# Value products a pair ahead of the sums over ones, and 59 pairs whose two addends TensorE adds, in an adaLN-attention-FFN kernel on one core

## What is computed

```python
def rational_softmax(scores, eps=EPS):
    num = 0.5 * (1.0 + scores * jax.lax.rsqrt(1.0 + scores * scores))
    return num / (jnp.sum(num, axis=-1, keepdims=True) + eps)
...
probs = rational_softmax(scores, EPS)
out = jnp.einsum('bhts,bhsd->bhtd', probs, v)
```

## Time and profile before

| | us |
|---|---|
| runs | 1978.49, 1980.25, 1984.89 |
| median | 1980.25 |
| the profiled execution | 1986.66 |
| its span, first to last instruction | 1984.9 |
| TensorE, VectorE, ScalarE, GpSimd busy | 1735.6, 1755.3, 1715.3, 1688.1 |
| mean granted clock of TensorE | 0.95 of full |

### The profile page before, as it was taken

The page is one execution under the profiler, slowest core; times in us unless marked ns, Lnnn a source line. Parts: engine busy times, 40 slices in busy tenths (PEclk is TensorE's granted clock), DMA queues, the critical chain, the costliest instruction groups (busy, mean ns, idle before and its releaser), DMA issues.

```text
span 1984.9 us, 29603 instructions
## 1 busy us (share of the span) xinstructions
PE 1735.6 (87%) x10668; PEld 884.6 (45%) x10671; DVE 1755.3 (88%) x1762; ACT 1715.3 (86%) x1853; POOL 1688.1 (85%) x720
## 2 busy tenths in 40 slices
PE   8898889998999889988988899889798887998786
PEld 6454346444555345633443444334343334443342
DVE  3988999899898988988899999898799988889887
ACT  2989999899898888999889998899889998899827
POOL 3878898889788878989889998899788988899875
PEclk9989999899899989989999999899999989999898
DMA  5322211322232333421421212212122213111155
GB/s 153 89 79 72 70 56 44 98 65 62 87 84 81 95 97 93 119 62 40 133 56 54 66 53 54 69 50 55 53 53 65 56 34 88 34 44 43 37 208 191
DMA packets 135326, 150.89 MB, mean 76 GB/s; under 512 B 32876, under 2 KB 76908, under 8 KB 134892
## 3 DMA queue, kind: packets, MB, share of 16 engines
q1 hardware_dynamic: 134604, 148.21, 26.5%
q10 hardware_dynamic: 576, 0.79, 0.2%
HBM read 57.44 MB, written 36.45 MB: 47 GB/s over the span
## 4 chain that ended last, share of the span: by engine, by line
PE 35%; ACT 24%; DVE 21%; issue 11%; SPq 4%; POOL 3%; DMA 2%; DVEq 0%; POOLq 0%; ACTq 0%
ACT yb L989 9%; DVE gb L1359 8%; PE sc L1196 7%; DVE gb L1431 7%; ACT yb L991 7%; PE ov L1171 6%; ACT gb L954 6%; PE dn L1171 5%; SPq L586 3%; PE it L1089 3%; PE it L1085 3%; PE it L1122 2%; PE it L1061 2%; PE it L1052 1%; PE sc L1199 1%
## 5 line engine op out<-in xcount | busy, mean ns | idle before, releaser
L911 POOL TENSOR_TENSOR yb<-yb 128x1024 f32<-128x1024 f32 x544 | 1495.9, 2761 | 252.1 <-DVE gb L1431 235.9
L1431 DVE TENSOR_TENSOR gb<-sc,yb 128x1024 f32<-128x1024 f32 x544 | 661.9, 1217 | 152.7 <-ACT yb L991 150.2
L1359 DVE TENSOR_TENSOR gb<-gb,yb 128x1024 f32<-128x1024 f32 x544 | 772.9, 1421 | 0.2
L989 ACT ACTIVATE yb<-sc 128x1024 f32<-128x1024 f32 x544 | 550.8, 1012 | 184.8 <-PE sc L1196 74.0
L1196 PE MATMUL sc<-qmv,kst 128*128 128x512 f32 (+3 forms) x1280 | 468.5, 448 | 154.3 <-DVE gb L1431 152.0
L991 ACT ACTIVATE yb<-yb 128x1024 f32<-128x1024 f32 x544 | 575.7, 1058 | 17.3
L954 ACT ACTIVATE gb<-gb 128x1024 f32<-128x1024 f32 x544 | 566.3, 1041 | 0.0
L1196 PEld LDWEIGHTS sc<-qmv,kst 128*128 128x128 f32 x1280 | 224.3, 198 | 458.6 <-DVE gb L1431 321.7
L1171 PE MATMUL ov<-gb,vv 128*32 128x512 f32 (+3 forms) x2560 | 319.1, 582 | 20.0 <-DVE oT L1379 14.5
L1171 PE MATMUL dn<-gb,ones 128*32 128x512 f32 (+3 forms) x2560 | 306.9, 562 | 0.0
L1085 PE MATMUL it<-hT,wT 128*128 128x512 f32 x488 | 238.9, 608 | 1.2 <-ACT area L966 1.2
(11 more groups left out here) (147 smaller groups left out, 1148.3 us busy)
## 6 DMA issues: line engine op xcount, KB each, us to landing
qmv<-stage SPq DMA_DIRECT2D x378, 64.0 KB
kst<-stage SPq DMA_DIRECT2D x372, 64.0 KB
area<-in_x_dram SPq DMA_DIRECT2D x50, 256.0 KB, 3.0
wf_d<-area SPq DMA_DIRECT2D x21, 256.0 KB, 2.0
wT<-wf_d SPq DMA_DIRECT2D x21, 256.0 KB, 3.0
h_d<-area SPq DMA_DIRECT2D x16, 256.0 KB, 3.3
hT<-h_d SPq DMA_DIRECT2D x4, 1024.0 KB, 7.2
o_d<-oT SPq DMA_DIRECT2D x4, 1024.0 KB, 6.7
```

What stands on the lines that cost most here:

```text
L911: pool.tensor_tensor(y, y, y, ALU.mult).then_inc(s_y2, 1)
L989: act.activation(yview(n), sc[:, n % SLOTS], ACT.Square).then_inc(s_s2, 1)
L1359: dve.tensor_tensor(gview(n), gview(n), yview(n), ALU.add).then_inc(s_num, 1)
L1431: dve.tensor_tensor(gview(n), sc[:, n % SLOTS], yview(n), ALU.mult).then_inc(s_g, 1)
```

## The change

1. `products` is split in two events: the value products "ov" stand at LAG = 5 pairs behind a unit's last pair, the sums over ones "dn" one pair later, where both stood. REGROUP, INVERT, ROWS and NORM are one more each, so that what hangs on dn keeps its pair.
2. A new function `by_load` picks pairs (TWICE) at least 8 apart, where its table of VectorE's work three pairs later is heaviest. The description says 58 of 544; the built program has 59. In these VectorE makes no sum: GpSimd writes y^2 into a buffer of its own, `square`, and TensorE multiplies both gb and `square`, accumulating both in the bank. The ring gb has 7 buffers, and `square` takes the place of the eighth.
3. `scored(k)` on VectorE and GpSimd comes at the next "qk" in any case, so VectorE's `hand_out` stands ahead of the product of its pair.
4. ScalarE waits for the square instead of the sum where the pair four back is in TWICE. The pieces of x1 that are loaded at the end are in another order: tiles 10 to 15 early, 0 to 5 and 6 to 9 late (before: 0 to 5 early, then 6 to 11 and 12 to 15).

```diff
-GRING = 8
+GRING = 7
 NUM_LAG = 2
-LAG = 6
-REGROUP = 1
-INVERT = 2
-ROWS = 3
-NORM = 6
+LAG = 5
+REGROUP = 2
+INVERT = 3
+ROWS = 4
+NORM = 7
+APART = 8
+BEFORE = 3
...
+        sums_at = {(k + 1) % n_pairs: u - n_units * ((k + 1) // n_pairs if u >= 0 else 0) for k, u in product_at.items()}
...
+            if k in sums_at:
+                self.events.append(("dn", sums_at[k]))
             if k in product_at:
-                self.events.append(("pv", product_at[k]))
+                self.events.append(("ov", product_at[k]))
...
+def by_load(groups):
+
+    weight = {"q": 1.4, "k": 1.4, "w2": 1.8, "fb": 0.4, "rt": 0.0, "a": 0.0, "zt": 0.0}
+    n_pairs = len(groups[0].pairs)
+    load = [0.0] * (len(groups) * n_pairs + LAG + 2)
+    for i, g in enumerate(groups):
+        for e in g.events:
+            if e[0] == "qk":
+                k = i * n_pairs + e[1]
+            elif e[0] == "item":
+                load[k] += weight.get(e[1].name[0], 0.65)
+                load[k + 1] += 0.7 * (e[1].name[0] == "zt")
+            elif e[0] == "step":
+                load[k] += 0.7 * (e[1].name[0] == "c8")
+        for last in g.last:
+            load[i * n_pairs + last + LAG + 1] += 1.3
...
+        best[n] = max(best[n + 1], load[n + BEFORE] + 0.3 + best[n + APART])
...
-        gb = sb("gb", [P, GRING, 2 * CH])
+        gb = sb("gb", [P, GRING + 1, 2 * CH])
...
+        SUMS = [(USED[1], KB), (0, USED[0]), (USED[0], USED[0] + 6), (USED[0] + 6, USED[1])]
...
+        square = gb[:, GRING, :].rearrange("p (h n) -> p h n", h=2)
...
                     pool.wait_ge(s_g, n + 1)
-                    pool.tensor_tensor(y, y, y, ALU.mult).then_inc(s_y2, 1)
+                    if n in TWICE and n != TWICE[0]:
+                        pool.wait_ge(s_pv, products_until(TWICE[TWICE.index(n) - 1]))
+                    pool.tensor_tensor(square if n in TWICE else y, y, y, ALU.mult).then_inc(s_y2, 1)
...
-                    if n >= YRING:
-                        act.wait_ge(s_num, n - YRING + 1)
+                    if n >= YRING and n - YRING in TWICE:
+                        act.wait_ge(s_y2, n - YRING + 1)
+                    elif n >= YRING:
+                        act.wait_ge(s_num, summed(n - YRING))
...
+            def addends(n):
+
+                return (gview(n), square) if n in TWICE else (gview(n),)
...
-                pe.wait_ge(s_num, n0 + len(plain.units[i]))
-                for dst, is_v in ((ov, True), (dn, False)):
-                    for n, p in pieces:
+                if is_v:
+                    for n in range(n0, n0 + len(plain.units[i])):
+                        if n in TWICE:
+                            pe.wait_ge(s_y2, n + 1)
+                            pe.wait_ge(s_g2, n + 1)
+                        else:
+                            pe.wait_ge(s_num, summed(n))
+                for n, p in pieces:
+                    for a, tile in enumerate(addends(n)):
                         lhsT = vv[:, p.kb, p.head * D:(p.head + 1) * D] if is_v else ones[:, :]
-                        r = pe.matmul(dst[p.head * D:(p.head + 1) * D, p.q0:p.q0 + p.width], lhsT,
-                                      gview(n)[:, p.bank, p.at:p.at + p.width], start=(p.kb == 0), stop=(i in g.last_unit))
-                r.then_inc(s_pv, 1)
+                        r = pe.matmul((ov if is_v else dn)[p.head * D:(p.head + 1) * D, p.q0:p.q0 + p.width], lhsT,
+                                      tile[:, p.bank, p.at:p.at + p.width], start=(p.kb == 0 and a == 0), stop=(i in plain.last_unit and a == (n in TWICE)))
+                if not is_v:
+                    r.then_inc(s_pv, 1)
...
             def numerator(n):
+                if n in TWICE:
+                    return
...
                 for e in g.events:
-                    if e[0] in ("qk", "pv") and k is not None:
+                    if e[0] == "qk" and k is not None:
                         scored(k)
-                        k = None
```

62 lines of the change are left out of this document (39 added, 23 removed).

## The result

| | before | after |
|---|---|---|
| median of 5 runs each, us | 1982.38 | 1971.20 |
| lowest to highest | 1978.49 to 1984.98 | 1965.87 to 1973.13 |
| after / before, 95% interval | | 0.9943 [0.9921, 0.9965] |
| loop over the 544 pairs | 1835.3 | 1817.8 |
| stretches at a granted clock of 0.50 (1.2 GHz) in it | 38, 177.4 us | 12, 61.5 us |

The change makes the kernel faster, by 11 us where 39 were forecast.

The account below looks back on a forecast made before the run. Four engines, 85 to 88% busy, take turns being late; a gain must come from ScalarE's 178 us idle in the loop. Terms -45 - 14 + 25 - 8 + 3 = -39 us gave 1941 us, range 1885 to 2009.

Parts of the forecast that it names:

- (a): Product block halved over two pairs: 7 in 10 clock falls go, -45 us; shorter waits for scores, -14 us.
- (b): TensorE's 253 more changes between full array and column strips: 0.2 us each, 51 us of TensorE work.
- (c): Second matmuls in the doubled pairs: 99 us of TensorE; with the strip changes 150 us, priced at +25 us.
- (d): VectorE spared 59 sums, 84 us of its work, but elsewhere than in full slices waiting anyway: -8 us.
- (e): New orders and waits, such as VectorE's product waiting for dn with a ring of 7: together +3 us.
- rival C: In the loop TensorE becomes the bound, needing 1773 of 1835 us: +38 us, 2018 us; chance 0.12.
- D: TensorE's matmuls in strict order, so a doubled pair costs twice as much: +29 us, 2009 us; chance 0.08.
- B: The falls of the clock in the loop stay: +5 us, 1985 us; chance 0.17.
- E: Larger gain: all clock falls go, other waits shrink, VectorE brings more: -94 us, 1886 us; chance 0.13.

Follow-up runs that it names:

- split_ring8: The kernel after with halved blocks but no doubled pair and a ring of 8: 1953.26 us, 0.9864 of before, -27.0 us.
- parted: The kernel before with ov moved right behind the scores and dn left at the end of the same pair, 213 more strip changes: 1.0085 of before, +16.9 us.
- doubled_summed: Halved blocks, ring of 8, no sum left out: TensorE multiplies 59 pairs twice while VectorE still forms all 544 sums: 1.0051 of before, +10.1 us.
- spared_only: Halved blocks, ring of 8: VectorE forms no sum in 59 pairs and TensorE multiplies nothing twice, y squared left out there: 0.9745 of before, -50.6 us.
- split_ring7: The kernel after with halved blocks and its ring of 7, but no doubled pair: 0.9902 of before, -19.4 us.
- before_ring7: The kernel before with a ring of 7 instead of 8 and the change's order of the last loads: 1.0048 of before, +9.5 us.
- after_ring8: The kernel after with a ring of 8; doubled pairs read gb twice, so y squared is left out there: 0.9947 of before, -10.5 us.
- twice_scored_empty: The kernel before with scores computed twice in the pairs that have no product block: 1.0139 of before, +27.6 us.
- before_lag5: The kernel before with its whole product block, ov and dn, one pair earlier, nothing halved or doubled: 0.9937 of before, -12.5 us.
- doubled_few: The kernel after with doubled pairs at least 24 pairs apart instead of 8, so 20 of them: 0.9879 of before, -24.0 us.
- doubled_some: The kernel after with doubled pairs at least 14 pairs apart instead of 8, so 34 of them: 0.9928 of before, -14.3 us.

## Why the prediction was right in sign and wrong in size

Each term of the sum, in us, as forecast and as the runs put it:

| term | forecast | measured | by |
|---|---|---|---|
| (a) halving, before the price of its changes | -59 | about -45, if (b) is 18 | split_ring8 -27, and 18 for (b) |
| (b) 253 changes | +8.5 (51 of the +25's 150) | about +18, not by itself | parted, 16.9 for 213; 0.28 us each, 0.25 on the path |
| (c) doubled matmuls | +16.5 (99 of 150) | +37 | doubled_summed |
| (d) VectorE spared | -8 | -24 | spared_only |
| (e) new waits and orders | +3 | +8 to +10 alone, nothing in the change | split_ring7, before_ring7, after_ring8 |
| sum | -39 | -14 to -6 | after: -11.3 |

By parts that were measured, halving with its changes was forecast at -50.5 and brought -27.0, 23.5 us less; the doubled pairs were forecast at +8.5 and cost 8.1 to 16.5. So most of the 28 us between forecast and result lies in the halving.

**(a), the step that failed first.** The prediction let halving take 7 in 10 of the falls and of the 63.7 us of ScalarE's idle time that go with them, -45. Halving took 16 of 38 falls, 4 in 10, and 22.7 of the 63.7 us (split_ring8). That 12 of 38 are left in the whole change, as the forecast of fewer than 15 has it, and that 41 us of such idle time went, is luck: the other ten falls went with the doubled pairs, whose added idle time elsewhere was larger. ScalarE's waits for scores, forecast under 80 us, are 100.1 with halving alone and 125.2 in the change.

The count of falls is no measure of the gain either. after has ten falls fewer than split_ring8 and is 16 us slower; twice_scored_empty has 15 fewer than before and is 28 us slower; before_lag5 has two more and is 12.5 faster. Where a quiet stretch is filled with work, the work is paid for elsewhere; where an engine is spared, as in spared_only (15 falls, -50.6), fewer falls and a gain go together. And of what halving brings, some 12 us may be the earlier place (before_lag5), which the prediction counted at nothing: it said that REGROUP, rows and norms keep their pairs, and overlooked that ov and its wait don't. (That the two parts add up was not tested.)

**(b), (c), the on-path share of TensorE's work: the second step that failed.** The amount was right: 122 to 177 us were given, and the loops show 1722.4 - 1622.9 = 99 us more busy time plus 58 for the slow time that went, 157. The share on the path was not. The prediction looked at 67 slices of eight pairs and counted as overflow only what a slice had no idle time for: 16 + 12 us, taken as 25. Measured, it is 37 for (c), and some 18 for (b) if parted's wait and place are let pass: 55. An eight-pair slice with 3 us of idle time is not a slice with 3 us to spare. As I read it (no run tests it by itself), the two score banks let TensorE run at most two pairs ahead of VectorE's product, so a matmul ahead of the scores delays ScalarE where the idle time lies more pairs away. The windows of the kernel after show where it ended; three of 26 slices (of 67) in which TensorE has less than 0.5 us idle, where the kernel before had 6:

```profile
128.40:155.50 27.10, 27.10 (x176) 14.99 (x174) 21.54 (x22) 23.18 (x24) 21.77 (x9) 1.00 0.22 61
155.50:182.70 27.20, 27.20 (x174) 13.71 (x170) 18.88 (x18) 22.01 (x23) 19.68 (x8) 1.00 0.22 60
...
454.00:481.10 27.10, 27.10 (x158) 12.64 (x162) 23.02 (x23) 24.92 (x26) 23.01 (x9) 1.00 0.27 70
```

In these three TensorE has no idle time at full clock, and none of the others is busy more than 92% of its slice: here TensorE is the bound. That is rival C's mechanism, which I priced as all or nothing from an idle time of 62 us on; it came in gradually, with 95 us idle.

**(d)** failed the same way with the other sign. VectorE's relief was counted at nothing where VectorE "was waiting anyway", and together with GpSimd's and the earlier release of yb it brought three times as much. Part of the size is that the relief was larger than 59 x 1.42 = 84 us: the sum's busy time fell from 772.9 to 658.7, by 114, since the remaining sums take 1358 ns instead of 1421. The two errors, +20.5 in (c) and -16 in (d), hid each other, by luck: the doubled pairs were forecast at +8.5 net and cost 8.1 (ring of 7) to 16.5 (ring of 8).

**(e).** The product's wait for dn was put under 20 us and is 64.6; the argument that it binds only at doubled blocks was wrong, since some 40 of its 69 times lie at plain ones, and split_ring7 has 32.2 us of it with no doubled pair. The ring of 7 costs 8 to 10 us where no pair is doubled, inside the bound of +20; that it is this wait that costs it is not shown. The hand-out's wait, 7.7 us, and the loads at the end (what lies ahead of the loop and behind it together went from 149.6 to 151.7 us) cost what was said, next to nothing. Whether the hand-out ahead of the product costs anything was not tried by itself.

**The rivals.** D, strict order, is ruled out. TensorE's timeline of the kernel after, doubled blocks of 12 records and a plain half block of 8:

```profile
527.18 1.93 PE L1231 MATMUL ov<-gb,vv 128*32 128x512 f32 x12
529.04 0.73 PE L1257 MATMUL sc<-qmv,kst 128*128 128x512 f32 x2
...
530.76 1.93 PE L1231 MATMUL dn<-gb,ones 128*32 128x512 f32 x12
...
535.32 1.07 PE L1231 MATMUL ov<-gb,vv 128*32 128x512 f32 x8
536.31 0.50 PE L1257 MATMUL sc<-qmv,kst 128*128 128x512 f32 x1
```

From a block's start to the next scores it is 1.86 us against 0.99: 0.87 more for the doubled one, as (c) took, and not 1.8 more. So it is for all of them: at full clock the 94 such blocks of 12 records with scores behind them take 1.85 to 1.86 us on the median, the 379 of 8 records 1.00. The Trainium skill, TensorE: Matmul & The Clock Gate, section The mechanism, has matmuls in strict program order; for matmuls in different column strips this trace does not agree, as far as the order in which the kernel writes them, both addends of a head side by side, is the order in which they were queued. B, the falls stay, is ruled out by the count, though its +5 us is nearer to the -11 measured than the forecast's -39. E is ruled out by the time. The counts named (ov and dn x2840, the sum x485) and the time of scores behind a half block were as forecast.

**The tests named in the prediction** were too lax. "TensorE's idle time below 60 us without a shorter loop" would have told only the extreme case; the chain's share of TensorE, 35 to 60%, and the unchanged waits for scores tell the actual one. What stays open: by which mechanism an earlier block gains, and what in the halved block brings the rest of its gain, 15 us of the 27 and what its changes cost, that neither the place nor the budget's evenness explains; and where the ring's 8 to 10 us arise.

## What to carry to other kernels

Where four engines are each 85% busy and hand every pair round, idle time is no cover: here a microsecond of added TensorE work cost 0.24 to 0.39 us in the places that were tried and one spared on VectorE, with what GpSimd gained by it, brought 0.26, so an exchange of one for the other (here 95 us of TensorE for 92 of VectorE) has to be priced at those rates before it is made. Measure the rate by one kernel that adds useless work to an engine, and move each part of a change by itself: this change held a gain of 27 us and two parts that took 16 of it back. A better granted clock is a symptom to read, not a gain to book.

## What the runs showed of the hardware that I had not expected

- **Fewer sums on VectorE go with shorter ones, and with shorter squares on GpSimd.** With 485 instead of 544 sums (spared_only), the mean sum takes 1380 ns against 1425 in split_ring8, and GpSimd's square 2666 against 2763: 52 us of GpSimd's and 22 us of VectorE's busy time beside the sums left out. With all sums formed and TensorE's work doubled (doubled_summed) they take 1399 and 2769, so the sum can get shorter by other things too, and the square did not. The square is 2733 ns with 524 sums (doubled_few) and 2705 with 510 (doubled_some). It has the same form in all of them and falls with the number of sums, which points to VectorE's sums beside it; by what means was not taken apart.

```profile
L958 POOL TENSOR_TENSOR yb<-yb 128x1024 f32<-128x1024 f32 x544 | 1445.3, 2666 | 247.7 <-DVE gb L1491 225.1
...
L1419 DVE TENSOR_TENSOR gb<-gb,yb 128x1024 f32<-128x1024 f32 x485 | 669.0, 1380 | 0.2
```

- **A change between four column strips and the full array and back costs TensorE 0.24 to 0.28 us** (61 us for 253, split_ring8; 59 for 213, parted), and, with what else changes in parted, 0.08 us of time (16.9 for 213).
- **Column strips run side by side, and a second matmul in one doesn't hold up the others**: the first four records of the block at 527.18 start within 0.03 us, and where two of the four strips get a second matmul, the 12 records take 0.87 us more than the 8 of a plain half block, which takes 1.07, and not 1.8 more.
